# Routed experts of a graph layer: row and gate gathers asked for earlier, 44 extra products on TensorE, two counts opened sooner

## The chip, the cores and the metric

The kernel runs on one core of one Trainium2 chip. The core has five engines with a queue of instructions each: TensorE (PE in the profile, its weight loads PEld), VectorE (DVE), ScalarE (ACT), GpSimd (POOL) and SyncE (SP). They wait for each other through semaphores. The metric is the device time in microseconds, the median of several runs.

## The reference

There are 3125 nodes with 256 features and 50,000 edges. A graph layer with attention over the edges comes first. Its result x then goes through a mixture of 16 experts, of which each node uses two. The part that the change touches:

```python
xn = layernorm(x)
probs = softmax(xn @ gate_w + gate_b)
top_probs, top_idx = top_k(probs, 2)
top_probs = top_probs / sum(top_probs)
hidden = silu(xn @ w1[e]) * (xn @ w2[e])      # for each of the 16 experts e
expert_out = hidden @ w3[e]
x = x + sum over e of dispatch[e] * expert_out[e]
```

The kernel computes for each node only its two experts.

## The kernel before

The first 765 us or so are the graph layer; nothing there is changed. Then comes the routing, and then the experts.

**Routing.** VectorE finds each node's two experts, and TensorE's `count` (two groups of products with triangular and all-one matrices) ranks the nodes within their experts. Nodes are sorted by expert into 64 blocks (`BLOCKS`) of 128 rows. VectorE and ScalarE build comparison matrices for five node tiles at a time (`high_hot`, `low_hot`, L1165 and L1169), TensorE multiplies them in 50 products (L1817), and the sum tells for each slot of a block which node stands in it. `done` (on TensorE) waits for the last product and sets the event `slot_sum`. VectorE then forms `slot_i` (L1177 to L1181) and sets `slots`. After that it works out which expert each block has (L1185 to L1188, event `experts`), copies the weights of blocks 0 and 1 (L1199), takes the difference of the two logits and sets `dl` (L1204, L1205), converts the block counts and sets `blocks` for SyncE's loop, and makes the gates (L1208 to L1216). ScalarE takes the exponential (L1543) behind `dl`; only behind that does it open its own counts `f_xt` and `f_si`. SyncE writes the gates to a table in memory (L1334).

**Counts and opening.** The pipeline of the experts uses semaphores of the class `Stage`: a waiter for block n waits for n + 9, and the owner adds 8 once when it "opens" the count. So even a wait for a block that does not exist (n below 0) holds until the owner has opened. TensorE opens `f_tx`, `f_h` and `f_y` behind the slots' products. VectorE opens `f_cw` before its first weight copy, and `f_hid` and `f_yc` only behind the gates (L1222 ff.).

**The experts, per block b.** GpSimd fetches the block's 128 rows with an indirect DMA (`gather_x`, L668) into one of `XB` = 3 buffers. TensorE transposes them (`turn_x`, L1828, 2 records) and ScalarE copies them out of PSUM (L1553). TensorE does `first_half` (L1839, 32 records: the products with w1 and w2). ScalarE takes the silu (L1558), VectorE the product of both halves (`gated`, L1226), TensorE does `second_half` (L1848, 8 records: w3). VectorE's `take_y` (L1233) scales the result by the gates and writes it to one of three buffers `y_st`; for that it waits for the block's gates, and for the addition of block b-3 to have landed, as that frees the buffer. GpSimd adds the 128 rows to the output with an indirect DMA (`scatter_y`, L678), and fetches the block's gates with another one (`gather_gates`, L672). Each addition waits for the landing of the one before.

**Order on the queues.** TensorE: `first_half(b)`, `turn_x(b+1)`, `second_half(b-1)`; the blocks 3 to 62 run in a loop whose body has 2 XB = 6 blocks. VectorE: `copy_weights(b+1)`, `gated(b)`, `take_y(b-1)`; every fourth `copy_weights` first reads registers. GpSimd: `gather_x(b+2)`, `gather_gates(b)`, `scatter_y(b-2)`; before block 0 it issues rows 0 and 1, and with block 0 it waits for the gate table. SyncE loads an expert's weights (L1324, L1326, 1.5 MB) into one of four places once the last block of the expert that had it is through: 12 such loads lie within the blocks.

Of the kernel before, what the change touches and what calls it, by code (L numbers as in the profile page):

```python
# [9 lines left out]
ALU = mybir.AluOpType  # L10
# [3 lines left out]
P = 128  # L14
N = 3125
D = 256
# [10 lines left out]
NT = NODE_TILES + 1  # L27
# [35 lines left out]
EPS = 1e-5  # L63
BLOCKS = (2 * N + NX * (P - 1)) // P
COPIED = 4
XB = 3
YB = 3
WX = 2 * KC * HID + HC * D
WB = 4
# [72 lines left out]
def build(nc, A, out):  # L142
    ctx = ExitStack()
    with ctx:
        def sb(name, shape, dt=F32):
            return ctx.enter_context(nc.sbuf_tensor(name, shape, dt))
# [4 lines left out]
        def sem(name):  # L151
            return ctx.enter_context(nc.semaphore(name))

        def dram(name, shape, dt=F32):
            return nc.dram_tensor(name, shape, dt, kind="Internal").ap()
# [18 lines left out]
        def event(name):  # L174
            if name not in events:
                events[name] = Event(sem("e_" + name))
            return events[name]
# [20 lines left out]
        gate_table = dram("gate_table", (NP * NX, 1))  # L198
# [9 lines left out]
        identb = sb("identb", [P, P], BF16)  # L208
        bias3 = sb("bias3", [3, 2, D], BF16)
        ones_b = sb("ones_b", [P, P], BF16)  # L210
# [16 lines left out]
        xinc_i = sb("xinc_i", [P, NX], I32)  # L227
# [75 lines left out]
        w_expert = flat[:, 0:WB * WX].rearrange("p (b n) -> p b n", b=WB)  # L303
        assert WB * WX + 2 * HID + XB * D + 2 * 2 * KC * HID <= 4 * LANE
        x2_all = acc
# [74 lines left out]
        top = sb("top", [P, NODE_TILES, 8])  # L380
# [15 lines left out]
        gates = sb("gates", [P, NODE_TILES, 2])  # L396
# [7 lines left out]
        slot_hi = sb("slot_hi", [P, BLOCKS])  # L404
        slot_f = sb("slot_f", [P, BLOCKS])
        gate_i = sb("gate_i", [P, BLOCKS], I32)
        gate_st = sb("gate_st", [P, YB, 1])
        row_at = sb("row_at", [P, 2])
        y_st = sb("y_st", [P, YB, D])

# [8 lines left out]

        xg = flat[:, WB * WX + 2 * HID:WB * WX + 2 * HID + XB * D].rearrange("p (b n) -> p b n", b=XB)  # L420
        w_block = flat[:, WB * WX + 2 * HID + XB * D:WB * WX + 2 * HID + XB * D + 2 * 2 * KC * HID].rearrange("p (b n) -> p b n", b=2)
        xg_t = sb("xg_t", [P, 2, D])
# [5 lines left out]
        bank = [qe_ps[0][:, 0:512], qe_ps[0][:, 512:1024], qe_ps[1][:, 0:512], qe_ps[1][:, 512:1024]] + [b[:, :] for b in rest_ps]  # L428
# [39 lines left out]
        f_cw, f_tx, f_xt, f_h, f_si, f_hid, f_y, f_yc = (Stage(sem(n)) for n in ("f_cw", "f_tx", "f_xt", "f_h", "f_si", "f_hid", "f_y", "f_yc"))  # L468
        s_wx, f_w = sem("s_wx"), Stage(sem("f_w"))
        s_xg = [sem(f"s_xg{i}") for i in range(XB)]  # L470
        s_ys = [sem(f"s_ys{i}") for i in range(YB)]
        s_gr = [sem(f"s_gr{i}") for i in range(YB)]
        s_gt = sem("s_gt")
        s_x3, s_w2, s_out = sem("s_x3"), sem("s_w2"), sem("s_out")
        s_pin = sem("s_pin")
# [79 lines left out]
        def _(pool):  # L555
            c = Chain(pool, s_pool)
# [109 lines left out]
            def gather_x(b):  # L666
                f_tx.wait(pool, b - XB)
                pool.indirect_dma_start(xg[:, b % XB, :], None, x3_table, bass.IndirectOffsetOnAxis(ap=slot_i[:, b:b + 1], axis=0)).then_inc(s_xg[b % XB], 16)  # L668

            def gather_gates(b):  # L670
                f_yc.wait(pool, b - YB)
                pool.indirect_dma_start(gate_st[:, b % YB, :], None, gate_table, bass.IndirectOffsetOnAxis(ap=gate_i[:, b:b + 1], axis=0)).then_inc(s_gr[b % YB], 16)  # L672

            def scatter_y(b):
                f_yc.wait(pool, b)
                if b:
                    pool.wait_ge(s_ys[(b - 1) % YB], 16 * ((b - 1) // YB + 1))
                pool.indirect_dma_start(out, bass.IndirectOffsetOnAxis(ap=slot_i[:, b:b + 1], axis=0), y_st[:, b % YB, :], None, compute_op=ALU.add).then_inc(s_ys[b % YB], 16)  # L678

            for b in range(XB - 1):  # L680
                gather_x(b)
            for b in range(BLOCKS):
                if b + XB - 1 < BLOCKS:
                    gather_x(b + XB - 1)
                if b == 0:
                    event("gate_rows").wait(pool)
                    pool.wait_ge(s_gt, 16)
                    pool.wait_ge(s_out, 16 * NT)
                gather_gates(b)
                if b >= 2:  # L690
                    scatter_y(b - 2)
            for b in range(BLOCKS - 2, BLOCKS):
# [5 lines left out]
        def _(v):  # L698
            c = Chain(v, s_dve)
# [443 lines left out]
            x_cnt, x_nb, x_inc, x_base = (xrow[:, i, :] for i in range(4))  # L1143
# [23 lines left out]
            def low_hot(m):  # L1167
                w = slice(m * SLOT_TILES, (m + 1) * SLOT_TILES)
                v.tensor_tensor(lo_hot[:, w, :, :], iota_b[:, :].unsqueeze(1).unsqueeze(1).to_broadcast([P, SLOT_TILES, 2, P]),  # L1169
                                lo_f[:, w, :].unsqueeze(3).to_broadcast([P, SLOT_TILES, 2, P]), ALU.is_equal).then_inc(r_lo.sem, 1)  # L1170
            high_hot(0)
            for m in range(NODE_TILES // SLOT_TILES):
                if m + 1 < NODE_TILES // SLOT_TILES:
                    high_hot(m + 1)
                low_hot(m)
            event("slot_sum").wait(v)
            c(v.tensor_copy(slot_hi[:, :], bank[5][:, 0:BLOCKS]))  # L1177
            c(v.scalar_tensor_tensor(out=slot_f[:, :], in0=slot_hi[:, :], scalar=float(P), in1=bank[5][:, BLOCKS:2 * BLOCKS], op0=ALU.mult, op1=ALU.add))
# [8 lines left out]
            c(v.tensor_scalar(be_i[:, :, 0], bef[:, :], float(NX - 1), None, ALU.min))  # L1187
            c(v.tensor_scalar(be_i[:, :, 1], be_i[:, :, 0], WB - 1, None, ALU.bitwise_and))  # L1188
            event("experts").set(v)
            f_cw.open(v)  # L1190


            def copy_weights(b):
                if b % COPIED == 0:
                    experts[:] = weights_of(mybir.EngineType.DVE, b, COPIED)
                e, w = experts[b % COPIED]
                f_w.wait(v, e)
                f_h.wait(v, b - 2)
                v.tensor_copy(w_block[:, b % 2, :], w[:, 0:2 * KC * HID]).then_inc(f_cw.sem, 1)  # L1199

            experts = []
            for b in range(2):
                copy_weights(b)
            c(v.tensor_tensor(gates[:, :, 1], top[:, :, 1], top[:, :, 0], ALU.subtract))  # L1204
            event("dl").set(v)  # L1205
            c(v.tensor_copy(xinc_i[:, :], x_inc))
            event("blocks").set(v)
            c(v.tensor_scalar(bef[:, :], bef[:, :], float(NX - 1), None, ALU.min))  # L1208
            c(v.scalar_tensor_tensor(out=gate_i[:, :], in0=slot_f[:, :], scalar=float(NX), in1=bef[:, :], op0=ALU.mult, op1=ALU.add))
            event("dexp").wait(v)  # L1210
# [6 lines left out]
            event("gates").set(v)  # L1217
            event("gate_rows").set(v)

            for s in (f_hid, f_yc):  # L1220
                s.open(v)

            def gated(b):
                f_si.wait(v, b)
                f_y.wait(v, b - 2)
# [1 line left out]

            def take_y(b):
                f_y.wait(v, b)
                v.wait_ge(s_gr[b % YB], 16 * (b // YB + 1))  # L1230
                if b >= YB:
                    v.wait_ge(s_ys[b % YB], 16 * (b // YB))
                v.tensor_scalar(y_st[:, b % YB, :], bank[6 + b % 2][:, 0:D], gate_st[:, b % YB, :], None, ALU.mult).then_inc(f_yc.sem, 1)  # L1233

            gated(0)
            for b in range(1, BLOCKS):
# [338 lines left out]
        def _(pe):  # L1575
# [170 lines left out]
            def done(ins, what):  # L1746
                pe_n[0] += 1
                ins.then_inc(s_pe, 1)
                pe.wait_ge(s_pe, pe_n[0])
                what.set(pe)  # L1750
# [24 lines left out]
            def gate(t):  # L1775
                g_ev.wait(pe, t)
                for k in range(KC):
                    ins = pe.matmul(logit_ps(t, t + 1), x2_t[:, t % 2, k * P:(k + 1) * P], gate_c[:, k, :], start=(k == 0), stop=(k == KC - 1))
                ins.then_inc(g_mm.sem, 1)

            def count(i):
                w = slice(*ROUTED[i])
                r_oh.wait(pe, i + 1)
                for j, a in enumerate((tri_b, ones_b)):
                    for k in range(2):
                        ins = pe.matmul(count_ps(i, j).rearrange("p (t x) -> p t x", x=NX), a[:, :], oh[:, w, k, :], start=(k == 0), stop=(k == 1))
                ins.then_inc(r_cnt.sem, 1)
# [7 lines left out]
            for t in range(NODE_TILES + TURNED + 1):  # L1795
                if t + 2 < NODE_TILES:
                    turn_rows(t + 2)
                if t < NODE_TILES:
                    new_rows_of(t)
                if 0 <= t - TURNED < NODE_TILES:  # L1800
                    turn_x2(t - TURNED)
                if t == TURNED:
                    event("gate_c").wait(pe)
                if 0 <= t - TURNED - 1 < NODE_TILES:
                    gate(t - TURNED - 1)
            event("tri").wait(pe)
            for i in range(2):
                count(i)

            slots = bank[5][:, 0:2 * BLOCKS]  # L1810
            for t in range(NODE_TILES):
# [4 lines left out]
                for k in range(2):  # L1816
                    ins = pe.matmul(slots, lo_hot[:, t, k, :], hi_hot[:, t, k, :, :].rearrange("p a b -> p (a b)"), start=(t + k == 0), stop=(t + k == NODE_TILES))  # L1817
            done(ins, event("slot_sum"))

            for s in (f_tx, f_h, f_y):  # L1820
                s.open(pe)
# [38 lines left out]
            with pe.Fori(0, (BLOCKS - 4) // (2 * XB)) as it:  # L1860
                for k in range(2 * XB):
                    b = it * (2 * XB) + 3 + k
                    i = (3 + k) % 2
# [37 lines left out]
```

## Time and profile before

| what | us |
|---|---|
| median of 3 runs (lowest, highest) | 1188.96 (1186.99, 1192.45) |
| profiled execution, its own time | 1188.13 |
| its span in the trace | 1186.4 |
| first `first_half` starts, last `take_y` starts | 810.90, 1173.65 |
| first and last addition are issued | 824.55, 1177.14 |

In the profile a line number such as L678 is the line of the kernel before. A row of a group gives the busy time and the mean duration, then the idle time of the engine just before these instructions and what ended it; "issue" is time in which the profile shows no wait. The tile names are those of the memory: the rows of a block stand under `ring`, the first PSUM banks under `qe_ps`. In rows in order of time the bracket tells the idle time before the first of the instructions and its releaser.

### The profile page before, as it was taken

Reading aid. Unit: us, or ns where it says so; the run is one execution under the profiler, and the core shown is the slowest. Engines: PE = TensorE matmul, PEld = TensorE weight load, DVE = VectorE, ACT = ScalarE, POOL = GpSimd, SP = SyncE. Lnnn points to the kernel's source line nnn. Section 1 sums busy time; section 2 is a strip of 40 time slices with the busy share of each in tenths; the row PEclk is TensorE's granted clock in tenths of the full one; section 3 lists DMA queues with packets and bytes.
Section 4 is the critical chain, followed back from the end, with each engine's and each line's share of the span. In section 5 each row is a group of like instructions: output and inputs, shape, how many; then the busy total and the mean of one; then the engine's idle time right before and its main releaser. Section 6 shows DMA issues by size and latency. Waiting matters only on the chain.

```text
span 1186.4 us, 23507 instructions
## 1 busy us (share of the span) xinstructions
PE 988.6 (83%) x6966; PEld 804.7 (68%) x6967; DVE 898.3 (76%) x1770; ACT 661.1 (56%) x2360; POOL 806.1 (68%) x777
## 2 busy tenths in 40 slices
PE   4988777888788788878887889826999999999995
PEld 1445555666566666656665656716999999989995
DVE  5868999999999999999999979994444444344441
ACT  3832568898998899898989746741111111111110
POOL 3648777777777777777777276404778775767783
PEclk9997978998999999999989989657999999999998
DMA  6346888888788888888887700463526436544332
GB/s 203 126 133 191 254 258 267 266 262 259 242 274 248 265 261 263 255 260 269 252 266 246 256 19 23 136 233 92 151 45 157 100 49 195 153 98 98 53 49 27
DMA packets 115036, 215.21 MB, mean 181 GB/s; under 512 B 21451, under 2 KB 59259, under 8 KB 114939
## 3 DMA queue, kind: packets, MB, share of 16 engines
q0 software_dynamic: 49536, 132.19, 39.3%
q1 hardware_dynamic: 63723, 80.57, 21.4%
q10 hardware_dynamic: 1680, 1.31, 0.4%
q8 instruction: 42, 0.69, 0.2%
q14 instruction: 55, 0.45, 0.1%
HBM read 191.47 MB, written 22.54 MB: 180 GB/s over the span
## 4 chain that ended last, share of the span: by engine, by line
PE 41%; DVE 24%; issue 14%; POOL 10%; DMA 5%; ACT 4%; DVEq 1%; SPq 1%; POOLq 0%; PEldq 0%; ACTq 0%
PE qe_ps L1839 14%; PE bank L1848 9%; POOL ring L604 8%; DVE ring L862 6%; PE bank L1839 5%; DVE ring L856 3%; PE qe_ps L1661 3%; DVE acc L874 2%; ACT wv L1442 2%; DMA ring<-kv_table,src_idx 2%; POOL ring L638 2%; PE bank L1701 2%; DVE score L868 2%; PE qe_ps L1589 1%; PE bank L1589 1%
## 5 line engine op out<-in xcount | busy, mean ns | idle before, releaser
L604 POOL DMA_INDIRECT ring<-kv_table,src_idx x440 | 427.8, 972 | 139.2 <-issue 126.5
L1442 ACT ACTIVATE wv<-ring,wgt 128x64 f32<-128x64 f32 x1628 | 406.9, 340 | 2.4 <-PE bank L1701 1.6
L1661 PE MATMUL qe_ps<-q,hot_t 128*128 x1320 | 200.2, 290 | 102.6 <-DVE ring L862 101.6
L1661 PEld LDWEIGHTS qe_ps<-q,hot_t 128*128 128x128 bf16 x1320 | 122.0, 103 | 152.3 <-issue 129.7
L1558 ACT ACTIVATE act<-qe_ps 128x512 f32<-128x512 f32 x64 | 38.2, 597 | 300.8 <-PE bank L1839 151.8
L1839 PEld LDWEIGHTS qe_ps<-xg_t,ring 128*128 128x128 f32 x1536 | 183.7, 194 | 7.2 <-issue 3.0
L1839 PE MATMUL qe_ps<-xg_t,ring 128*128 128x128 f32 x1536 | 184.3, 277 | 3.4 <-DVEq L102 2.6
L1701 PE MATMUL bank<-wv,hotf 128*128 128x260 f32 x588 | 163.9, 408 | 6.2 <-DVE acc L874 6.2
L678 POOL DMA_INDIRECT out<-y_st,slot_i x64 | 114.2, 1785 | 60.9 <-DMA out<-y_st,slot_i 34.8
L862 DVE TENSOR_TENSOR ring<-ring,qe_ps 128x512 f32<-128x512 f32 x220 | 149.3, 679 | 0.2
L856 DVE TENSOR_TENSOR ring<-ring,bank 128x1024 f32<-128x1024 f32 x110 | 133.6, 1215 | 5.6 <-DMA ring<-kv_table,src_idx 5.0
L868 DVE TENSOR_REDUCE score<-ring 128x16 f32<-128x1024 f32 x110 | 133.6, 1214 | 0.2
L1701 PEld LDWEIGHTS bank<-wv,hotf 128*128 128x128 f32 x588 | 108.5, 201 | 24.3 <-DVE acc L874 9.8
L1848 PE MATMUL bank<-ring 128*128 x512 | 121.5, 380 | 1.7 <-issue 1.1
L668 POOL DMA_INDIRECT ring<-x_table,slot_i x64 | 75.4, 1178 | 55.1 <-DVEq L125 35.9
L1848 PEld LDWEIGHTS bank<-ring 128*128 128x128 f32 x512 | 92.3, 190 | 12.9 <-issue 3.0
L672 POOL DMA_INDIRECT gate_st<-gate_table,gate_i x64 | 79.8, 1247 | 28.6 <-issue 16.4
L1226 DVE TENSOR_TENSOR ring<-act,qe_ps 128x512 f32<-128x512 f32 x32 | 22.0, 688 | 84.8 <-ACT act L1558 84.8
L1199 DVE COPY ring<-ring 128x2048 f32 x64 | 79.5, 1243 | 8.3 <-issue 8.3
L1701 PE MATMUL qe_ps<-wv,hotf 128*128 128x260 f32 x292 | 82.6, 408 | 2.6 <-DVE acc L874 2.4
L1226 DVE TENSOR_TENSOR ring<-act,bank 128x512 f32<-128x512 f32 x32 | 22.0, 688 | 77.5 <-ACT act L1558 77.5
L1436 ACT ACTIVATE hotf<-bank 128x512 f32<-128x512 bf16 x110 | 60.2, 587 | 22.3 <-PE bank L1676 10.0
(332 smaller groups left out, 1548.1 us busy)
## 6 DMA issues: line engine op xcount, KB each, us to landing
ring<-in_w SPq DMA_DIRECT2D x48, 512.0 KB, 5.0
d_row<-d_rows SPq DMA_DIRECT2D x55, 256.0 KB
t_row<-t_rows SPq DMA_DIRECT2D x55, 256.0 KB
ring<-kv_table,src_idx POOLq DMA_INDIRECT x440
kv_table<-ring SPq DMA_DIRECT2D x25, 256.0 KB, 2.0
out<-acc SPq DMA_DIRECT2D x26, 128.0 KB, 1.7
x_table<-ring SPq DMA_DIRECT2D x26, 128.0 KB, 1.8
ring<-in_x SPq DMA_DIRECT2D x12, 256.0 KB, 9.0
```

The lines of the kernel that those rows point to most:

```text
L604: pool.indirect_dma_start(ring[:, u, place(g) * D:(place(g) + 2) * D], None, kv_table, bass.IndirectOffsetOnAxis(ap=src_idx[:, 4 * g + u:4 ...
L672: pool.indirect_dma_start(gate_st[:, b % YB, :], None, gate_table, bass.IndirectOffsetOnAxis(ap=gate_i[:, b:b + 1], axis=0)).then_inc(s_gr ...
L678: pool.indirect_dma_start(out, bass.IndirectOffsetOnAxis(ap=slot_i[:, b:b + 1], axis=0), y_st[:, b % YB, :], None, compute_op=ALU.add).the ...
L856: v.tensor_tensor(k, k, rel_ps[:, at:at + 4 * HD].rearrange("p (u d) -> p u d", u=4).unsqueeze(2).to_broadcast([P, 4, H, HD]), ALU.add).th ...
L862: v.tensor_tensor(k, k, q_ps[p % AHEAD].rearrange("p (u c) -> p u c", u=2), ALU.mult).then_inc(a_prod.sem, 1)
L868: v.tensor_reduce(s, by_head(k_rows(g)), AX.X, ALU.add).then_inc(a_red.sem, 1)
L1199: v.tensor_copy(w_block[:, b % 2, :], w[:, 0:2 * KC * HID]).then_inc(f_cw.sem, 1)
L1442: ins = act.activation(wv[:, g % WV_N, u, h, 0:HD], v_rows(g)[:, u, h * HD:(h + 1) * HD], ACT.Copy, scale=w[:, col:col + 1])
L1661: ins = pe.matmul(q_ps[p % AHEAD][:, u * D:(u + 1) * D], hot_t[:, p // 4 % HB_N, hot_cols(p, u)], tile_of(q3, q_tiles[p % 4])[:, k * D:(k ...
L1701: ins = pe.matmul(task_bank(("sum", p))[:, 0:H * HB], hotf[:, g % HF_N, u, :], wv[:, g % WV_N, u, :, :].rearrange("p h d -> p (h d)"), sta ...
L1839: ins = pe.matmul(bank[1 + 2 * m + i][:, h * P:(h + 1) * P], w_block[:, i, at:at + P], xg_t[:, i, c * P:(c + 1) * P], start=(c == 0), stop ...
L1848: ins = pe.matmul(bank[6 + i][:, 0:D], hid_t[:, i, c * P:(c + 1) * P], w[:, at:at + D], start=(c == 0), stop=(c == HC - 1))
```

## The change

`gather_x` gets six buffers (`XB` = 6): five blocks' rows are asked for before block 0, and rows are asked for five blocks ahead. `gate_st` gets six places of its own (`GB` = 6); four gathers of gates are issued before block 0 and the others four blocks ahead. The wait for the gate table stands ahead of all gathers of gates. TensorE's loop gets bodies of 12 blocks. `idle_products` puts 24 products of 128x512 into bank 7 behind `count`, and 20 behind `slot_sum` ahead of the opening of TensorE's counts; nobody reads them. On VectorE the difference with `dl` and the conversion with `blocks` move ahead of the wait for `slot_sum`; `f_hid` and `f_yc` are opened with `f_cw`, ahead of the first weight copies.

```diff
-XB = 3
+XB = 6
+GB = 6
+GATES = 4
...
             def gather_gates(b):
-                f_yc.wait(pool, b - YB)
+                f_yc.wait(pool, b - GB)
...
             for b in range(XB - 1):
                 gather_x(b)
+            event("gate_rows").wait(pool)
+            pool.wait_ge(s_gt, 16)
+            for b in range(GATES):
+                gather_gates(b)
+            pool.wait_ge(s_out, 16 * NT)
             for b in range(BLOCKS):
                 if b + XB - 1 < BLOCKS:
                     gather_x(b + XB - 1)
-                if b == 0:
-                    event("gate_rows").wait(pool)
-                    pool.wait_ge(s_gt, 16)
-                    pool.wait_ge(s_out, 16 * NT)
-                gather_gates(b)
+                if b + GATES < BLOCKS:
+                    gather_gates(b + GATES)
                 if b >= 2:
                     scatter_y(b - 2)
...
+            c(v.tensor_tensor(gates[:, :, 1], top[:, :, 1], top[:, :, 0], ALU.subtract))
+            event("dl").set(v)
+            c(v.tensor_copy(xinc_i[:, :], x_inc))
+            event("blocks").set(v)
             event("slot_sum").wait(v)
...
             event("experts").set(v)
-            f_cw.open(v)
+            for s in (f_cw, f_hid, f_yc):
+                s.open(v)
...
             for b in range(2):
                 copy_weights(b)
-            c(v.tensor_tensor(gates[:, :, 1], top[:, :, 1], top[:, :, 0], ALU.subtract))
-            event("dl").set(v)
-            c(v.tensor_copy(xinc_i[:, :], x_inc))
-            event("blocks").set(v)
...
+            def idle_products(n):
+                for _ in range(n):
+                    pe.matmul(bank[7].rearrange("p (i c) -> p i c", i=4), identb[:, :], ones_b[:, :].unsqueeze(1).to_broadcast([P, 4, P]), start=True, stop=True)
+
             for i in range(2):
                 count(i)
+            idle_products(24)
...
             done(ins, event("slot_sum"))
+            idle_products(20)
             for s in (f_tx, f_h, f_y):
                 s.open(pe)
```

## Rows read from the trace of the kernel before

**Rows 1.** Page, busy times of the engines over the whole span.

```profile
PE 988.6 (83%) x6966; PEld 804.7 (68%) x6967; DVE 898.3 (76%) x1770; ACT 661.1 (56%) x2360; POOL 806.1 (68%) x777
```

**Rows 2.** Groups by line, 800 to 1186 us: busy, mean ns; idle before, its enders.

```profile
L678 POOL DMA_INDIRECT out<-y_st,slot_i x64 | 114.2, 1785 | 60.9 <-DMA out<-y_st,slot_i 34.8 <-issue 17.2 <-DVE y_st L1233 8.8
...
L672 POOL DMA_INDIRECT gate_st<-gate_table,gate_i x64 | 79.8, 1247 | 28.6 <-issue 16.4 <-DMA gate_table<-cm 9.4 <-DMA out<-y_st,slot_i 1.8
...
L668 POOL DMA_INDIRECT ring<-x_table,slot_i x64 | 75.4, 1178 | 55.1 <-DVEq L125 35.9 <-issue 16.8 <-PE qe_ps L1828 2.4
```

**Rows 3.** Table of stretches: us, busy per engine (count), TensorE clock, DMA share, GB/s.

```profile
812.00:815.00 3.00, 3.00 (x16) 3.00 (x16) 0.00 (x0) 0.01 (x1) 0.00 (x0) 0.50 0.83 111
```

**Rows 4.** Order of time, 789 to 825 us: start, us, engine, line, operation.

```profile
789.87 1.25 PE L1817 MATMUL bank<-hi_hot,q 128*128 128x128 bf16 x10 [12.68 <-DVE q L1169]
...
799.06 0.23 DVE L1177 COPY slot_hi<-bank 128x64 f32<-128x64 f32 x1 [1.44 <-PEq L125]
...
800.66 1.94 POOL L668 DMA_INDIRECT ring<-x_table,slot_i  x1 [35.86 <-DVEq L125]
...
804.57 2.37 DVE L1199 COPY ring<-ring 128x2048 f32 x2 [1.16 <-issue]
...
807.63 0.66 PE L1828 MATMUL qe_ps<-ident,ring 128*128 128x128 f32 x2 [8.69 <-ACTq L102]
...
810.49 0.37 SPq L1334 DMA_DIRECT2D gate_table<-cm  x1
...
810.90 6.10 PE L1839 MATMUL qe_ps<-xg_t,ring 128*128 128x128 f32 x32 [2.62 <-DVEq L102]
...
815.28 0.94 POOL L672 DMA_INDIRECT gate_st<-gate_table,gate_i  x1 [9.37 <-DMA gate_table<-cm]
...
823.79 0.48 DVE L1233 TENSOR_SCALAR y_st<-bank,gate_st 128x256 f32<-128x256 f32 x1 [0.63 <-PE bank L1848]
824.19 1.22 DVE L1199 COPY ring<-ring 128x2048 f32 x1
824.55 2.37 POOL L678 DMA_INDIRECT out<-y_st,slot_i  x1 [2.43 <-DVE y_st L1233]
```

**Rows 5.** Chain that ended last, one block: start, us, what.

```profile
823.75 3.57 PE qe_ps L1839 x32
827.32 0.22 PE qe_ps L1828 x2
827.54 1.73 PE bank L1848 x8
```

**Rows 6.** The tile y_st: its writers and readers over the span, DMA landings.

```profile
L1233 DVE TENSOR_SCALAR y_st<-bank,gate_st x64: 483/484/485, 823.8 to 1173.6; 128x256 f32<-128x256 f32 x64
...
DMA to landing us min/median/max: 3.7/3.9/8.3
```

**Rows 7.** Order of time around loads of experts' weights, SyncE, VectorE, GpSimd.

```profile
987.09 0.90 SPq L1324 DMA_DIRECT2D ring<-in_w  x2
...
1067.46 0.89 SPq L1324 DMA_DIRECT2D ring<-in_w  x2
1067.65 1.22 DVE L1199 COPY ring<-ring 128x2048 f32 x1
1067.84 2.52 POOL L678 DMA_INDIRECT out<-y_st,slot_i  x1 [0.35 <-DVE y_st L1233]
...
1075.50 1.61 POOL L678 DMA_INDIRECT out<-y_st,slot_i  x1 [2.58 <-DMA out<-y_st,slot_i]
```

**Rows 8.** Order of time, a gather that meets VectorE's copy.

```profile
1139.38 1.22 DVE L1199 COPY ring<-ring 128x2048 f32 x1
1139.42 2.03 POOL L668 DMA_INDIRECT ring<-x_table,slot_i  x1 [0.30 <-issue]
```

**Rows 9.** Chain that ended last, its last pieces.

```profile
1172.64 3.75 DMA out<-y_st,slot_i
...
1177.14 1.55 POOL out L678
```

More of the change, by code:

```diff
@@ L406, in build @@
         gate_i = sb("gate_i", [P, BLOCKS], I32)
-        gate_st = sb("gate_st", [P, YB, 1])
+        gate_st = sb("gate_st", [P, GB, 1])
         row_at = sb("row_at", [P, 2])
@@ L471, in build @@
         s_ys = [sem(f"s_ys{i}") for i in range(YB)]
-        s_gr = [sem(f"s_gr{i}") for i in range(YB)]
+        s_gr = [sem(f"s_gr{i}") for i in range(GB)]
         s_gt = sem("s_gt")
@@ L670, in gather_gates @@
             def gather_gates(b):
-                f_yc.wait(pool, b - YB)
-                pool.indirect_dma_start(gate_st[:, b % YB, :], None, gate_table, bass.IndirectOffsetOnAxis(ap=gate_i[:, b:b + 1], axis=0)).then_inc(s_gr[b % YB], 16)
+                f_yc.wait(pool, b - GB)
+                pool.indirect_dma_start(gate_st[:, b % GB, :], None, gate_table, bass.IndirectOffsetOnAxis(ap=gate_i[:, b:b + 1], axis=0)).then_inc(s_gr[b % GB], 16)
             def scatter_y(b):
@@ L1218, in _ @@
             event("gate_rows").set(v)
-            for s in (f_hid, f_yc):
-                s.open(v)
             def gated(b):
@@ L1229, in take_y @@
                 f_y.wait(v, b)
-                v.wait_ge(s_gr[b % YB], 16 * (b // YB + 1))
+                v.wait_ge(s_gr[b % GB], 16 * (b // GB + 1))
                 if b >= YB:
                     v.wait_ge(s_ys[b % YB], 16 * (b // YB))
-                v.tensor_scalar(y_st[:, b % YB, :], bank[6 + b % 2][:, 0:D], gate_st[:, b % YB, :], None, ALU.mult).then_inc(f_yc.sem, 1)
+                v.tensor_scalar(y_st[:, b % YB, :], bank[6 + b % 2][:, 0:D], gate_st[:, b % GB, :], None, ALU.mult).then_inc(f_yc.sem, 1)
             gated(0)
```

## The prediction

> **What bounds the kernel now.** The page says TensorE, busy 83% of the span [rows 1], and the chain that ended last agrees from 811 us on: a block is 3.57 + 0.22 + 1.73 = 5.52 us of products without a gap [rows 5]. But an average hides who is nearly as full. So I read the groups by line for the experts' stretch next, for what ended GpSimd's idle time [rows 2]. GpSimd issues per block one gather of rows (mean 1.18 us), one of gates (1.25) and one addition (1.79), each with 0.3 us of issue: 5.1 us of 5.52. And of the 60.9 us it idled before additions, 34.8 went to the landing of the addition before and only 8.8 to waiting for a result, 2.4 of these before the first and 3.5 before the last but one. GpSimd is thus late for almost the whole stage, and only TensorE's lead of buffers hides it. Its additions run from 824.55 to 1177.14 [rows 4, 9], 5.60 us apart on average. The results run from 823.79 to 1173.65 [rows 6]; 62 steps of 5.52 and a last of 1.77 make 344, so 5.8 us of stalls are in the 349.8. The kernel ends 9.3 us of span after the last addition is issued (1186.4 - 1177.14), whatever TensorE did.
>
> **The change, part by part.** The sum is made against the profiled execution, 1188.13 us (span 1186.4), which lies 0.8 us under the median of 1188.96.
>
> *24 products behind the counts.* TensorE idles 12.7 us ahead of the slots' first products, and ten of these, of 128 columns, take 1.25 us at the half clock [rows 4], so one of 512 columns is estimated at 0.43 us, 24 at 10.3. They fit: 0. If they kept the clock up until the slots' last ten products, these would gain 0.6; I take 0.
>
> *20 products behind the slots.* They end 4.3 us (full clock) to 8.6 us (half) after 799.0, at 803.3 to 807.6; I take 806. The clock stood at half, 1.2 GHz, through most of the first half of block 0, which so took 6.10 us instead of 3.57 [rows 3 to 5]. I take that the products bring it to 2.4 GHz: 2.5 us. The opening of `f_tx`, which holds GpSimd's first gather, now stands behind them on TensorE's queue. If it goes with the queueing of the products, it costs nothing, since the gather starts at 800.66 anyway; if with their end, the first gather moves up to 7 us back. I take the first, as registers read between products leave no gap in TensorE's chain [rows 5].
>
> *Events and counts on VectorE.* The transpose of block 0 waited until 807.63 for ScalarE's opening, behind `dl`, and its products until 810.90 for VectorE's opening behind the gates [rows 4]. Both go. The moved operations (estimated at 0.5 us with their signals) fit into the 1.4 us that VectorE idles for the slots' sum [rows 4]; the two openings put an estimated 0.2 us ahead of the copies. What is late next is the end of the 20 products: transpose and ScalarE's copy behind 806, first half at about 807, where the copied weights have been ready since about 806. So the first half starts 3.9 us sooner and is 2.5 shorter; the first result is ready at 823.75 - 6.4 = 817.3. The gate table is written 0.4 us sooner, and gates can be gathered from 814.9 instead of 815.28.
>
> *GpSimd's order.* Before its first addition it now issues ten gathers behind the gate table (4 gates, then 3 rows and 3 gates in turn): 7 x 1.55 + 3 x 1.48 = 15.3 us, so the first addition goes at about 830 instead of 824.55, 12.7 us behind its result instead of 0.8. Nothing is removed from GpSimd; three gathers of rows and four of gates only move ahead of the additions. That is a point against the change: its scarce engine starts its chain 5.5 us later.
>
> *The rings.* Rows and gates asked for earlier are never late: the 5.8 us of stalls, as far as rows or gates made them, go. But `y_st` still has three buffers. Result b + 3 comes 16.5 us behind result b and needs addition b landed, 3.9 us at the median after its issue [rows 6]; with 12.7 + 3.9 = 16.6 VectorE now waits for landings from the first block on. TensorE doesn't stall until an addition lags its result by some 15.5 us, as a weight copy (1.2 us) and a write (0.5) are still in hand.
>
> *Where the copy falls.* This decides. An addition restarts 0.75 us behind the landing of the one before (1172.64 + 3.75 to 1177.14, [rows 9]); without a copy beside it additions are 4.5 to 4.7 us apart. VectorE, released by the same landing, starts its copy about 0.5 us behind it (the write takes 0.4 until the copy starts, [rows 4]). So the addition is issued some 0.3 us into the copy. A gather that did so took 2.03 us instead of 0.99 [rows 8], an addition 0.2 us into one 2.52 instead of 1.63 [rows 7]: here about +0.8, so 5.3 to 5.5 us apart, 5.4. Every fourth copy starts 0.4 us later, behind register reads, and lets its addition through at about 4.9; mean 5.3. Before, lag drifted the copy over all three instructions.
>
> The Trainium skill, SBUF — State Buffer, section "Who interferes with whom", says that a VectorE copy in its two-port mode and GpSimd exclude each other for the whole instruction, whoever comes first. The trace agrees for GpSimd (2.03 us beside 0.99), but not the other way round: copies that found GpSimd at work took 1.22 us as well. By the page's rule read strictly, copies would wait for a whole addition, and TensorE's margin would be gone sooner, toward the slower rival below.
>
> *Experts' weights.* An addition under way at such a load lands only with it: 8.0 us from the load's issue to the next addition [rows 7]. Twelve loads come in the stage. With block 0's lag the first one (block 2 ready, 828.4) catches addition 0, and addition 1 goes at 837. The others cost a lone one 0.3 to 1 us, those that follow each other 2.9 each (8.3 to 9.3 us from one to the next, of which the one at 987.09 stands in [rows 7], with another 8.3 before and 9.3 behind it; two more at 1030 and 1039); together some 17 us, bounds 8 and 30.
>
> *Sum.* Addition 1 at 837; 59 steps of 5.3 = 313; loads 17; last three steps of 4.6 = 14: the last addition at 1181, 4 later than 1177.14. **1188.1 + 4 = 1192 us.** TensorE's gain of 12 us ends in waiting for buffers.
>
> **Rivals.**
> *A, TensorE stays the bound (chance 0.14).* Everything is 6.4 us sooner and 5.8 us of stalls go: 1188.1 - 12.2 = 1176. For it: the chain of waits names TensorE nearly throughout. Against it: GpSimd's row of idle times [rows 2]. It holds if steps come to 5.0 us or less.
> *B, the additions lock at TensorE's pace (0.28).* With steps of 5.5, and loads that catch additions which started just ahead of them, TensorE is held too: 59 x 0.2 = 12 more less what the tail gives back, about 1201. It decides from a step of 5.45 us. For it: landing and copy hang on one event, so the clash repeats by itself.
> *C, the clock or the opening fails (0.06).* If the products don't raise the clock, or the first gather waits for their end, TensorE's gain is 3 to 6 us instead of 12. As GpSimd's chain starts at the gate table, the end is the forecast's, 1190 to 1193. The skill's TensorE: Matmul & The Clock Gate, section "Why this matters for your kernels", asks for dense products without long idle gaps; the row at the half clock with TensorE fully busy [rows 3] shows that being busy lifts it only after a while.
>
> **How the numbers follow.** The forecast case has 0.52, 1186 to 1198 (steps 5.25 to 5.4, loads 10 to 25). Less than 0.5%, 5.9 us, can't be told from no change. Faster (under 1183) is A and hardly more: 0.15. Slower (over 1195) is B with part of the forecast case: 0.38. The rest, 0.47, is within. The range, 1182 to 1203, leaves out A's core and B's end.
>
> **What would show it.** First half of block 0 at about 807 and 3.6 us long (opening, clock). First addition at about 830. VectorE's idle time before `take_y` ended by additions' landings in most blocks, additions of 2.4 us in three of four, their last at about 1181. TensorE's stalls around 990 to 1050 ended by VectorE's copies and no more by rows. The prediction is wrong if additions follow their results by under 11 us through the middle, or if no landing holds VectorE.

## The result, and the profile after

The changed kernel takes 1197.23 us in the median (8 runs, 1194.48 to 1201.32), the kernel before 1188.68 beside it (8 runs, 1185.65 to 1192.57): a ratio of 1.0076, 95% interval 1.0056 to 1.0097. It is slower by 8.5 to 9 us. The forecast was 1192, with 1182 to 1203 as the range: a change of 4 us where 8.5 to 9 came. The profiled execution took 1199.05 us, 10.9 more than that of before.

The groups by line of the experts' stretch of the changed kernel, with the columns of [rows 2] (L680 additions, L674 gates, L670 rows, L1235 `take_y`, L1208 weight copies, L1848 the first half's products):

```profile
L1848 PE MATMUL qe_ps<-xg_t,ring 128*128 128x128 f32 x1536 | 187.3, 280 | 13.2 <-DVE ring L1208 12.2 <-ACT xg_t L1555 0.7
...
L680 POOL DMA_INDIRECT out<-y_st,slot_i x64 | 136.7, 2136 | 77.2 <-DVE y_st L1235 57.9 <-DMA out<-y_st,slot_i 15.8 <-issue 3.5
...
L1208 DVE COPY ring<-ring 128x2048 f32 x64 | 78.7, 1231 | 8.2 <-issue 7.8 <-PE bank L1848 0.4
L670 POOL DMA_INDIRECT ring<-x_table,slot_i x64 | 66.6, 1040 | 55.1 <-DVEq L127 35.9 <-issue 16.8 <-PE qe_ps L1837 2.4
...
L674 POOL DMA_INDIRECT gate_st<-gate_table,gate_i x64 | 62.2, 971 | 25.5 <-issue 25.2 <-DMA out<-y_st,slot_i 0.3
...
L1235 DVE TENSOR_SCALAR y_st<-bank,gate_st 128x256 f32<-128x256 f32 x64 | 30.9, 483 | 146.7 <-DMA out<-y_st,slot_i 134.0 <-PE bank L1857 8.7 <-DMA gate_st<-gate_table,gate_i 4.0
```

Against [rows 2]: an addition takes 2.14 us instead of 1.79, a gather of rows 1.04 instead of 1.18, one of gates 0.97 instead of 1.25. The three together are as long as before, 4.15 to 4.21 us; the delay by VectorE's copies has only moved onto the additions. VectorE waits 134 us for additions to land before it writes a result, and TensorE 12.2 us for copies, which stand behind those writes on VectorE's queue.

The start, in order of time, as [rows 4]:

```profile
799.60 6.01 PE L1811 MATMUL bank<-ones_b,identb 128*128 128x512 bf16 x20
...
801.28 1.84 POOL L670 DMA_INDIRECT ring<-x_table,slot_i  x1 [35.94 <-DVEq L127]
...
806.82 3.81 PE L1848 MATMUL qe_ps<-xg_t,ring 128*128 128x128 f32 x32 [0.99 <-DVE ring L1208]
...
815.51 0.95 POOL L674 DMA_INDIRECT gate_st<-gate_table,gate_i  x1 [6.33 <-issue]
...
820.79 0.48 DVE L1235 TENSOR_SCALAR y_st<-bank,gate_st 128x256 f32<-128x256 f32 x1 [4.01 <-DMA gate_st<-gate_table,gate_i]
...
829.24 2.36 POOL L680 DMA_INDIRECT out<-y_st,slot_i  x1 [0.30 <-DVE y_st L1235]
...
838.52 2.45 POOL L680 DMA_INDIRECT out<-y_st,slot_i  x1 [4.33 <-DVE y_st L1235]
```

The first half of block 0 starts 4.1 us sooner and takes 3.81 us instead of 6.10; the first addition goes 4.7 us later than in [rows 4].

Two blocks from the stretch in which VectorE waits for landings, VectorE and GpSimd in order of time:

```profile
866.54 0.48 DVE L1235 TENSOR_SCALAR y_st<-bank,gate_st 128x256 f32<-128x256 f32 x1 [1.33 <-DMA out<-y_st,slot_i]
866.94 1.22 DVE L1208 COPY ring<-ring 128x2048 f32 x1
867.21 2.45 POOL L680 DMA_INDIRECT out<-y_st,slot_i  x1 [0.87 <-DVE y_st L1235]
...
872.11 0.48 DVE L1235 TENSOR_SCALAR y_st<-bank,gate_st 128x256 f32<-128x256 f32 x1 [1.45 <-DMA out<-y_st,slot_i]
872.77 1.61 POOL L680 DMA_INDIRECT out<-y_st,slot_i  x1 [0.56 <-DVE y_st L1235]
873.02 1.23 DVE L1208 COPY ring<-ring 128x2048 f32 x1 [0.43 <-issue]
```

One landing releases the write; copy and addition follow it. The addition is issued 0.27 us into the copy and takes 2.45 us. In the next block VectorE has read registers (0.43 us of "issue"), the copy comes 0.25 us behind the addition's start, and the addition takes 1.61. The name after the arrow for the addition is only the event that the profile saw last.

TensorE behind its first and its longest long gap, products in order of time, and then the table of stretches around the first, with the columns of [rows 3]:

```profile
852.82 5.44 PE L1848 MATMUL qe_ps<-xg_t,ring 128*128 128x128 f32 x32 [1.93 <-DVE ring L1208]
...
1018.89 3.81 PE L1848 MATMUL qe_ps<-xg_t,ring 128*128 128x128 f32 x32 [2.86 <-DVE ring L1208]
```

```profile
848.00:850.00 2.00, 2.00 (x16) 1.90 (x15) 0.00 (x0) 0.87 (x2) 0.95 (x1) 1.00 1.06 283
850.00:852.80 2.80, 0.89 (x5) 0.45 (x4) 1.83 (x3) 0.00 (x0) 1.60 (x1) 1.00 1.01 355
...
854.00:856.00 2.00, 2.00 (x12) 2.00 (x11) 0.81 (x2) 0.00 (x0) 1.20 (x3) 0.50 0.47 104
...
858.00:860.00 2.00, 2.00 (x13) 1.82 (x12) 0.69 (x1) 0.87 (x2) 1.39 (x3) 1.00 0.55 63
```

TensorE had been full at 2.4 GHz, stood for 1.93 us, and 1.2 us after it began again the granted clock was 1.2 GHz for a while; the work behind it came 3.8 us late for a gap of 1.93, as its first half took 5.44 us and not 3.81. The gaps before 996.74 (2.22 us) and 1055.17 (2.79) did the same, 4.1 and 4.7 us. The longest, 2.86 us before 1018.89, did not: the granted clock stayed at 2.4 GHz from 1019 to 1026, and it cost 3.1 us. TensorE's last result is ready 18.6 us behind an unbroken 5.52 us a block; 5.8 in the kernel before.

The last pieces of the chain of waits, as [rows 9]:

```profile
1172.96 0.49 DVE y_st L1235
...
1182.74 3.67 DMA out<-y_st,slot_i
...
1187.16 1.56 POOL out L680
```

The last addition is issued 10.0 us later than in [rows 9]. From there to the end of the span it is 10.1 us instead of 9.2: GpSimd's last instruction, a drain, takes 5.95 us in the trace, 4.93 before.

Seven of the experiments ran on chips on which the kernel before itself takes 1416 to 1418 us instead of 1187, the experts beginning only at 1020 to 1034 us; for these the experts' stretch is compared, from the first gather of rows to the end of the span: 385.7 us before (800.66 in [rows 4] to 1186.4), 396.0 after. Neither the kernel before nor the changed one was traced on those chips, so these comparisons cross chips and rest on one execution each. The one kernel traced on both kinds, e11 and e12 below, differs by 2.9 us, and six of the seven runs there have a pause of TensorE of 0.8 to 5.2 us around the third block that the runs on the other chips do not have. A difference of 3 us between stretches is no finding.

### The profile page after: what moved, and what is told of

Same layout as the page of the kernel before. It is cut to its first block, busy times and chain, and to the rows that moved or that the text cites. A ratio compares the mean times of both kernels' runs of the same rounds, so it can differ in the third digit from the quotient of the medians.

```text
span 1197.3 us, 23560 instructions
## 1 busy us (share of the span) xinstructions
PE 1007.3 (84%) x7010; PEld 811.1 (68%) x7011; DVE 895.4 (75%) x1770; ACT 660.1 (55%) x2360; POOL 801.5 (67%) x777
## 3 DMA queue, kind: packets, MB, share of 16 engines
q10 hardware_dynamic: 1680, 1.31, 0.4%
## 4 chain that ended last, share of the span: by engine, by line
PE 24%; DVE 21%; DMA 18%; issue 17%; POOL 15%; ACT 2%; DVEq 2%; SPq 0%; POOLq 0%; PEldq 0%; ACTq 0%
DMA out<-y_st,slot_i 14%; POOL ring L606 14%; PE qe_ps L1848 7%; DVE ring L866 5%; PE bank L1857 4%; DVE acc L878 3%; DVE ring L860 2%; DMA ring<-kv_table,src_idx 2%; PE bank L1848 2%; PE qe_ps L1767 1%; PE bank L1703 1%; PE qe_ps L1591 1%; DVE y_st L1235 1%; PE bank L1591 1%; DVE score L872 1%
## 5 line engine op out<-in xcount | busy, mean ns | idle before, releaser
L1848 PEld LDWEIGHTS qe_ps<-xg_t,ring 128*128 128x128 f32 x1536 | 184.6, 196 | 20.6 <-issue 16.8
L1848 PE MATMUL qe_ps<-xg_t,ring 128*128 128x128 f32 x1536 | 187.3, 280 | 13.2 <-DVE ring L1208 12.2
L680 POOL DMA_INDIRECT out<-y_st,slot_i x64 | 136.7, 2136 | 77.2 <-DVE y_st L1235 57.9
L1235 DVE TENSOR_SCALAR y_st<-bank,gate_st 128x256 f32<-128x256 f32 x64 | 30.9, 483 | 146.7 <-DMA out<-y_st,slot_i 134.0
L1703 PEld LDWEIGHTS bank<-wv,hotf 128*128 128x128 f32 x588 | 108.0, 201 | 25.2 <-DVE acc L878 10.9
L670 POOL DMA_INDIRECT ring<-x_table,slot_i x64 | 66.6, 1040 | 55.1 <-DVEq L127 35.9
L1857 PEld LDWEIGHTS bank<-ring 128*128 128x128 f32 x512 | 92.3, 190 | 10.1 <-issue 0.2
L1208 DVE COPY ring<-ring 128x2048 f32 x64 | 78.7, 1231 | 8.2 <-issue 7.8
L674 POOL DMA_INDIRECT gate_st<-gate_table,gate_i x64 | 62.2, 971 | 25.5 <-issue 25.2
L878 DVE TENSOR_TENSOR acc<-acc,bank 128x260 f32 x147 | 61.1, 416 | 3.4 <-PE bank L1703 1.7
```

The costliest lines, as they stand in the source:

```text
L878: v.tensor_tensor(a, a, task_bank(("sum", pair))[:, 0:H * HB], ALU.add).then_inc(b_acc.sem, 1)
L1703: ins = pe.matmul(task_bank(("sum", p))[:, 0:H * HB], hotf[:, g % HF_N, u, :], wv[:, g % WV_N, u, :, :].rearrange("p h d -> p (h d)"), sta ...
L1848: ins = pe.matmul(bank[1 + 2 * m + i][:, h * P:(h + 1) * P], w_block[:, i, at:at + P], xg_t[:, i, c * P:(c + 1) * P], start=(c == 0), stop ...
L1857: ins = pe.matmul(bank[6 + i][:, 0:D], hid_t[:, i, c * P:(c + 1) * P], w[:, at:at + D], start=(c == 0), stop=(c == HC - 1))
```

## The experiments

**e1: six buffers for results.** `YB = 3` becomes `YB = 6`; to make room for their semaphores, three others of the kernel are shared.

> The changed kernel with y_st in six buffers instead of three. Theory (the additions lock to the copies because VectorE waits for an addition's landing before it writes a result and copies right behind): VectorE is held by no landing up to a lag of some 32 us, results come every 5.52 us from 817.4 and end near 1162; the copies drift over GpSimd's instructions, additions fall from a mean of 2.14 to about 1.8 us, and end near 1166: 1172 to 1182 us, 1176. Rival (the late first addition and GpSimd's own queue set the end, whatever VectorE waits for): additions stay at 2.4 us in three of four, the last near 1185: 1193 to 1198.

Measured: 1190.86 us, ratio to before 1.0030 (1.0013 to 1.0048); stretch 389.2.

```profile
L679 POOL DMA_INDIRECT out<-y_st,slot_i x64 | 111.5, 1742 | 71.8 <-DMA out<-y_st,slot_i 47.6 <-issue 15.9 <-DVE y_st L1234 8.2
...
L673 POOL DMA_INDIRECT gate_st<-gate_table,gate_i x64 | 78.6, 1228 | 25.6 <-issue 21.6 <-DVE y_st L1234 2.1 <-DMA out<-y_st,slot_i 1.8
L669 POOL DMA_INDIRECT ring<-x_table,slot_i x64 | 73.8, 1153 | 55.1 <-DVEq L127 35.9 <-issue 18.3 <-PE qe_ps L1836 0.9
L1234 DVE TENSOR_SCALAR y_st<-bank,gate_st 128x256 f32<-128x256 f32 x64 | 30.9, 484 | 47.6 <-PE bank L1856 43.3 <-DMA gate_st<-gate_table,gate_i 4.3
```

No landing holds VectorE any more and the additions are short, but neither theory gave the time. The last result is written at 1166.3, and the last addition goes only at 1178.5. Here and below, how far an addition is behind its result is counted from the end of VectorE's write. In order of time, from the middle:

```profile
921.26 1.22 DVE L1207 COPY ring<-ring 128x2048 f32 x1
921.30 2.00 POOL L673 DMA_INDIRECT gate_st<-gate_table,gate_i  x1 [0.30 <-issue]
923.60 1.62 POOL L679 DMA_INDIRECT out<-y_st,slot_i  x1 [0.30 <-issue]
925.53 0.98 POOL L669 DMA_INDIRECT ring<-x_table,slot_i  x1 [0.30 <-issue]
926.78 1.22 DVE L1207 COPY ring<-ring 128x2048 f32 x1
926.82 2.00 POOL L673 DMA_INDIRECT gate_st<-gate_table,gate_i  x1 [0.31 <-issue]
```

GpSimd waits for nothing here: 2.00 + 1.62 + 0.98 and three times 0.30 are 5.50 us, TensorE's own pace. The copy now falls on the gather of gates, and the additions stay 18.6 to 19.2 us behind their results over eight blocks (11 to 18). The hold by landings costs some 5.5 us (ratios 1.0076 and 1.0030). What stays is that GpSimd, with one copy on its instructions in every block, can hardly catch up at all. The theory was revised to that before the next runs.

**e2: the start alone.** Rows, gates and GpSimd's order of before (`XB = 3`, gates with their block), with the 44 products and VectorE's moves.

> The kernel before with TensorE's 44 products and VectorE's moved counts and openings; rows, gates and GpSimd's order as before. Theory: results start 6.4 us sooner, the first addition at about 821.5, the stalls of before (5.9 us) stay, no landing holds VectorE: 1180 to 1186 us, 1182. Rival (the products or the moved openings cost as much as they bring): 1187 to 1191.

Measured: 1182.59 us, ratio 0.9962 (0.9949 to 0.9975); stretch 380.1. As the theory had it, and by a ratio wholly under 1. The first addition goes at 822.70, 0.28 us behind its result, and additions follow results by 3.4 us in the median of blocks 8 to 50 (11.2 in the changed kernel).

**e3: the rings alone.** The diff's lines on `XB`, `GB`, `GATES` and GpSimd's order, nothing else.

> The kernel before with six buffers of rows and of gates and GpSimd's new order alone, no idle products, nothing moved on VectorE. Theory: the first addition comes near 829 us as in the changed kernel, the same chain of additions with the same loads follows: 1191 to 1199 us, 1195, although TensorE starts 6.4 us later than there. Rival (the order costs nothing, the start does): 1187 to 1190.

Measured: 1191.41 us, ratio 1.0037 (1.0023 to 1.0050); stretch 387.5.

```profile
L680 POOL DMA_INDIRECT out<-y_st,slot_i x64 | 120.6, 1884 | 65.9 <-DMA out<-y_st,slot_i 31.8 <-DVE y_st L1237 23.9 <-issue 10.2
...
L1237 DVE TENSOR_SCALAR y_st<-bank,gate_st 128x256 f32<-128x256 f32 x64 | 30.9, 484 | 85.5 <-DMA out<-y_st,slot_i 60.0 <-PE bank L1857 25.5
```

The first addition goes at 828.92 as in the changed kernel, but only 4.75 us behind its result, since TensorE starts late here. Landings hold VectorE for 60 us instead of 134, and make no result late before block 32. The start alone brings 4.5 us, the rings alone cost 4.4; together they should cost nothing, and cost 9. The two parts work against each other: the sooner TensorE's results come, the farther behind them the additions stand, and the sooner the three buffers are full.

**e4: without the idle products.** Both calls of `idle_products` go.

> The changed kernel without its 44 products; all else as in it. Theory: the clock stands at half in the first half of block 0, which takes 6.1 us, the first result is ready 2 to 3 us later; the additions start at the gate table all the same and set the end: 1195 to 1199 us, no difference. Rival (TensorE's start sets the end): 1200 to 1203.

Measured: 1196.09 us, ratio 1.0081 (1.0061 to 1.0100).

```profile
804.28 6.71 PE L1846 MATMUL qe_ps<-xg_t,ring 128*128 128x128 f32 x32 [1.18 <-DVE ring L1208]
```

The products make the first half of block 0 2.9 us shorter (6.71 without them, at 1.2 GHz until 810, and 3.81 with them), and the end does not move, as the theory had it.

**e5: another order on VectorE.**

```diff
-                if b + 1 < BLOCKS:
-                    copy_weights(b + 1)
                 gated(b)
+                if b + 1 < BLOCKS:
+                    copy_weights(b + 1)
                 take_y(b - 1)
```

> The changed kernel with VectorE's order in a block gated, copy, take_y instead of copy, gated, take_y: the copy starts some 0.7 us later behind the write that a landing releases, so an addition that goes 0.75 us behind its landing starts before the copy. Theory after six buffers (GpSimd's queue is full: each copy makes one of its three instructions of the block some 0.8 to 1.0 us longer, wherever it falls; the hold by landings only chooses the addition): the clash moves to the gather of rows behind it, additions fall to 1.6 us but the step stays at 5.2 to 5.5: 1189 to 1196 us. Rival (the clash with the addition is what costs): steps of 4.7, additions catch up with the results, 1178 to 1184.

Measured: stretch 447.6 us (ratio 1.0458 in the whole, 1.0417 to 1.0500). Both missed.

```profile
L1848 PE MATMUL qe_ps<-xg_t,ring 128*128 128x128 f32 x1536 | 190.7, 282 | 57.4 <-DVE ring L1208 56.7 <-ACT xg_t L1555 0.7
```

`gated(b)` waits for the silu of block b, so the copy for b + 1 now begins behind the first half of b and is not done when TensorE wants it: a stall of some 0.9 us in every block. Additions did fall to 1.62 us in the mean, but at a pace of 6.5 us a block, slower than either kind of step, this decides nothing between the two.

**e6: no loads among the blocks.** The call of `load_expert` in SyncE's loop goes, its count is raised at once; the later blocks so use old weights.

> The changed kernel with the twelve loads of experts' weights during the experts' stage left out (blocks beyond the fourth expert multiply old weights, so the output differs). Theory: additions held by loads lose some 22 us of delay; the lag of the additions never reaches 15 us, TensorE is never held, its clock never falls, results end near 1162: 1173 to 1178 us. Rival (the steps between loads, not the loads, hold the chain): 1188 or more.

Measured: stretch 381.7 us, 14.3 less than after. (The whole: ratio 0.9987, 0.9960 to 1.0013, that is 1.8 us under before where the changed kernel is 9 over it; by this the loads cost some 11.)

```profile
L680 POOL DMA_INDIRECT out<-y_st,slot_i x64 | 105.3, 1646 | 36.8 <-issue 17.8 <-DVE y_st L1235 13.0 <-DMA out<-y_st,slot_i 5.9
...
L1235 DVE TENSOR_SCALAR y_st<-bank,gate_st 128x256 f32<-128x256 f32 x64 | 31.0, 484 | 44.4 <-PE bank L1857 36.7 <-DMA gate_st<-gate_table,gate_i 4.0 <-remote 3.7
```

Without loads the late start is caught up and no landing holds VectorE for long; additions follow by 2.3 us. Beginning where the changed kernel begins, this would be 1184.7 us (801.3 + 381.7 + 1.7 around the span) and not the 1173 to 1178 expected; 5.2 us of that are one gap of TensorE near the start, at a wait for `xg_t`, the longest of the pauses named above. Both the theory's range and its rival's (1188 or more) were missed.

**e8 and e9: copies on ScalarE.** The copies leave VectorE; ScalarE makes them behind its two operations of a block. e8 is the changed kernel with that, e9 the start alone (e2) with that. VectorE's gates come sooner, as they stood behind two copies, and ScalarE's loop is written out.

```diff
+                act.activation(w_block[:, b % 2, :], w[:, 0:2 * KC * HID], ACT.Copy).then_inc(f_cw.sem, 1)
...
+            for b in range(BLOCKS):
+                silu(b, b % 2)
+                if b + 1 < BLOCKS:
+                    copy_xt(b + 1, (b + 1) % 2)
+                if b + 2 < BLOCKS:
+                    copy_weights(b + 2)
```

> The changed kernel with the copies of the experts' weights made by ScalarE, behind its own two operations of a block, instead of by VectorE. Theory (GpSimd's instructions are held by VectorE's copies): gathers stay at 0.95 to 1.0 us, additions at 1.6, steps without a load fall to 4.7; the lag of 15 us at the start is gone by the middle, and TensorE's pace sets the end: 1173 to 1180 us. Rival (additions held by landings and by the late start, not by copies): 1188 to 1194.

> The kernel with the start alone (44 products, moved counts and openings; rows, gates and GpSimd's order of before) and the copies made by ScalarE. Theory: additions follow their results closely, the stalls of 5.2 us that rows made go, results end near 1162 and the last addition goes near 1165: 1173 to 1177 us. Rival (ScalarE's copies, longer than VectorE's, hold TensorE or its transposes' copies): 1182 or more.

Measured: stretches 380.4 and 379.0 us (the whole: 0.9969, 0.9944 to 0.9994, and 0.9974, 0.9946 to 1.0003). The one change takes 15.6 us out of the changed kernel's stretch, 13 by the whole times against before; with additions that start on time (e9 against e2's 380.1) it takes 1 us, which is no finding. By the same sum that is 1183 and 1182 us, over both ranges: in e8 TensorE has pauses of 3.6 us together in the first 30 us that the profile gives to no wait (none in e12, below), in e9 a stall of 1.90 us by rows stays, in one place.

```profile
L680 POOL DMA_INDIRECT out<-y_st,slot_i x64 | 103.5, 1618 | 72.9 <-DMA out<-y_st,slot_i 32.8 <-DVE y_st L1224 23.0 <-issue 17.0
L670 POOL DMA_INDIRECT ring<-x_table,slot_i x64 | 64.4, 1006 | 55.1 <-DVEq L127 36.0 <-issue 11.3 <-PE qe_ps L1830 7.9
L674 POOL DMA_INDIRECT gate_st<-gate_table,gate_i x64 | 60.9, 952 | 50.8 <-DVE y_st L1224 33.1 <-issue 14.4 <-DMA out<-y_st,slot_i 3.3
```

These are e8's. The three instructions now take 3.58 us a block, 0.6 less than before or after, and additions released by landings are 4.6 us apart.

**e9b: e9 once more.**

> The kernel of e9 once more, in an undisturbed run. Its experts' stage, from the slots' numbers to the end, took 379.6 us against 386.3 in the kernel before and 380.7 with the start alone. Theory (ScalarE's copies leave GpSimd alone; without a late start of the additions this only shortens what loads delay): 1178 to 1184 us, some 1 us under the start alone. Rival (the longer copies on ScalarE cost TensorE elsewhere): over 1185.

Measured: stretch 379.4 us, ratio 0.9982 (0.9949 to 1.0015). It fell on such a chip again: the stretch repeats, the whole stays unclear.

**e10: one block of gates ahead.** `GATES = 4` becomes 1 in the changed kernel.

> The changed kernel with gates one block ahead instead of four; five blocks of rows, six buffers and all else kept. Three gathers fewer (3.7 us) stand ahead of the first addition. Theory (GpSimd's queue is nearly full, so the end moves with the first addition): the first addition at about 26 us behind the slots' numbers instead of 28.6, the end 2 to 4 us sooner: 1192 to 1196 us. Rival (the additions stick at a place relative to the copies whatever their start): 1196 to 1199.

Measured: stretch 389.3 us, 6.7 less than after (the whole: 1.0015, 0.9988 to 1.0042). The first addition goes 24.3 us behind the slots' numbers instead of 28.6. The end follows the first addition, by more than the theory asked. The ratios of the whole, 1.0015 and 1.0076, have intervals that do not meet and say the same; only the direction is safe.

**e11 and e12: both.** e8 with `GATES = 1`, the same kernel twice.

> The changed kernel with the copies on ScalarE and gates one block ahead. Theory: GpSimd has 0.8 us a block to spare, catches up from the late first addition within some ten blocks, and rows asked for five blocks ahead take away the stalls of 2 to 3 us that rows make; TensorE's pace sets the end: 1176 to 1182 us, the fastest of all. Rival (six more counters at the end and early loads eat it): 1182 to 1186, no faster than the start with scalar copies.

> The kernel of e11 once more (copies on ScalarE, gates one block ahead). Its experts' stage, from the slots' numbers to the end, took 377.7 us against 386.3 in the kernel before. Theory: the gain of 8 to 9 us stands in the whole as well: 1176 to 1182 us where the kernel before takes 1187 to 1189, a ratio of 0.992 to 0.994. Rival (the stage's gain came from that one execution): 0.996 or more.

Measured: stretch 377.0 us, ratio 0.9945 (0.9917 to 0.9972); and **1175.65 us, ratio 0.9912 (0.9893 to 0.9931)**, stretch 374.1. e11 lies within its range by the sum used for e6 (1180 us); e12 is slightly under its own. The rows of e12:

```profile
L1841 PE MATMUL qe_ps<-xg_t,ring 128*128 128x128 f32 x1536 | 182.0, 275 | 2.0 <-ACT xg_t L1542 2.0
L1555 ACT ACTIVATE ring<-ring 128x2048 f32 x64 | 122.3, 1912 | 9.2 <-issue 9.2
L680 POOL DMA_INDIRECT out<-y_st,slot_i x64 | 103.6, 1618 | 93.9 <-DMA out<-y_st,slot_i 42.3 <-DVE y_st L1224 39.2 <-issue 12.4
...
1161.77 0.48 DVE L1224 TENSOR_SCALAR y_st<-bank,gate_st 128x256 f32<-128x256 f32 x1 [1.29 <-PE bank L1850]
1165.31 1.56 POOL L680 DMA_INDIRECT out<-y_st,slot_i  x1 [2.99 <-DMA out<-y_st,slot_i]
```

TensorE has no gap over 0.3 us behind the first two blocks; no stall by rows is left, with rows asked for early. It beats both kernels, the changed one by 1.6% (the two ratios to before divided).

## Why the prediction came out as it did

**Right.** *The start:* the 24 products took 7.7 us and hid, the 20 ended at 805.6 (forecast 806), the first gather of rows went with the opening at their queueing (801.28, beside them), the clock was up, the first half started at 806.82 (807). *GpSimd's order:* ten gathers, first addition at 829.24 (830). *The hold:* VectorE waits for landings 48 times, from block 3 on. Counted from the time at which TensorE has a result ready, as the forecast counted, the first addition is 11.9 us behind (12.7) and the median of blocks 8 to 50 is 14.2, none under 11, so that the sign of being wrong did not come. *Where the copy falls:* additions take 2.2 to 2.6 us in 41 blocks, mostly 2.45, three of four where no load is near; four steps from 1092.41 to 1113.53 are 5.28 each (forecast 5.3). Rival A (1176) fell: GpSimd's row of idle times was the better guide than the chain of waits. Rival B did not come about between loads, where steps stayed at 5.28 in the mean of a group of four, below its 5.45. By the number alone it could not be told apart: the measured 1197 lies nearer to its 1201 than to 1192, and only the steps and the loads decide for the forecast's account. Rival C fell by the first gather's start and by e4's comparison.

**Mis-sized: the loads.** The forecast's 59 steps were 313 for the steps and 17 for the loads; they took 335.1, of which loads are 335.1 - 59 x 5.28 = 23.6. The error is in the lone loads, taken at 0.3 to 1 us. The kernel before has two kinds of them: at the loads at 890, 912 and 940 us its steps were 5.59, 5.92 and 6.11 us, at those at 851, 1008 and 1067 they were 7.62, 7.22 and 7.66. The forecast took the price of the first kind for all, and here all were of the second. The lone ones issued at 888, 910 and 938 us now made steps of 8.27, 7.12 and 7.26 us, and those at 846, 1011 and 1074 steps of 7.24, 7.99 and 7.29: 1.8 to 3.0 each over 5.28. Those that follow each other, taken at 2.9, cost 2.7 in the mean. 23.6 is within the bounds of 8 to 30 that the forecast gave. Addition 1 went at 838.5 and not 837. With 0.5 gained at the tail this is the last addition at 1187.2 instead of 1181.

**Missed: the end.** 0.9 us from the last addition to the end, taken as unchanged. With it, 3.9 + 6.1 + 0.9 makes the 10.9 us between the two profiled executions. Both errors go the same way: the range held the result, but the outcome was "slower (over 1195)", which had 0.38, and the change is over twice the one forecast.

**Missed, without effect: the first result's gates.** The first result was ready at 817.4 as forecast, but was written at 820.79, as its gates, asked for at 815.51, landed only then, beside a load of 1.5 MB. The first addition was later anyway.

**Half right: TensorE.** "TensorE's gain of 12 us ends in waiting for buffers": it did, and the long stalls are ended by copies, as said. That such a stall can also bring the clock down, three of the four times here, for 1.9 us more each, was not foreseen. It did not set the end here: additions were behind throughout.

**A reading of the kernel before that was wrong in part.** The prediction says that copies that found GpSimd at work took 1.22 us as well. Most did, but 9 of the 64 there took 1.31 to 1.49 us; the last section has the rows of the changed kernel. The estimate of 0.43 us for a product of 512 columns does not follow from its source either: ten products of 128 in 1.25 us make 0.50, and 12.0 us for 24. Neither moved the sum.

**What the theory had wrong.** The prediction made the meeting of landing and copy the point that decides. e1 shows it to be 5.5 us of 9. Below it lies a plainer cause, shown by e8 and e12: one copy of VectorE in a block delays one of GpSimd's three instructions by 0.4 to 1.0 us where it meets one, and so takes nearly all that GpSimd could catch up with. A late first addition is then late at the end too (e10), and every load adds to it (e6). That the additions in e1 kept one distance from the copies for eight blocks was seen; why was not tested.

## What to carry to other kernels

Asking earlier is not free on an engine that is nearly full: ten gathers ahead of the first addition moved the whole chain of additions. Add up what the issuing engine does in a block, with the delays others put on it, before it is given work ahead of its critical instruction; if the delay can be moved to an engine with room (here copies of 1.23 us on VectorE became 1.91 us on ScalarE), do that first; then the deeper buffers may pay. Rows asked for early made no stall of TensorE in e11 and e12, where e9 and e9b, without them, had one of 1.5 to 1.9 us; what they are worth in time is not shown, as e9 was never timed on the chips of e12. Two parts of a change that bring and cost 4.5 us alone can cost 9 together, if one lets the producer run ahead and the other holds the consumer back.

## What the runs showed of the hardware

- Three stalls of TensorE of 1.93, 2.22 and 2.79 us in the midst of full work were followed by a stretch at 1.2 GHz, in which a first half took 5.44 us instead of 3.81. A fourth of 2.86 us was not, and in e4 one of 3.17 us was and two of 2.10 and 1.88 us were not: the length of the stall alone does not tell.
- The last drain of GpSimd takes 4.93 us in before and e2, where the experts' indirect DMAs raise nine counters, and 5.95 us in the changed kernel with 15; but 5.99 in e1 with 18, so it is no simple price by the counter. Every other run agrees: 4.93 in e9 and e9b with nine, 5.95 in all with 15.
- A copy of VectorE and an instruction of GpSimd held each other, GpSimd by far the more. Beside a copy, gathers took up to 2.0 us instead of 0.95 to 0.99 and additions up to 2.6 instead of 1.6. Most copies took 1.22 us all the same, but where a gather that no earlier copy held had begun 0.6 to 0.7 us ahead, the copy took 1.30 to 1.40 us and the gather kept its own time. The longest copy, beside an addition, took 1.53. Two rows of the changed kernel show it:

```profile
820.52 0.94 POOL L670 DMA_INDIRECT ring<-x_table,slot_i  x1 [0.30 <-issue]
...
821.19 1.32 DVE L1208 COPY ring<-ring 128x2048 f32 x1
```

The Trainium skill, SBUF — State Buffer, section "Who interferes with whom", says that the two exclude each other, and that whoever issues first has the shared ports for the whole instruction. The trace agrees that either can be kept out, but not that the start of the instruction decides: in e1 a gather of gates that had begun 0.46 us ahead of the copy still took 1.80 us, while the copy took 1.23.
